# A graph network on one Trainium2 core: the node path's output bias moves from a VectorE add to one-row matmuls in the gather stage

## The reference, cut to what matters

```python
x = h @ W_in.T + b_in
x = jax.nn.silu(x)
x = _linear_diffusion(x, src, dst)
x = x @ W_out.T + b_out
...
x = _layernorm(x + _L3_gnn_ref(...), axis=-1)
```

## Time and profile before

| what | value |
|---|---|
| median of three runs | 3779.49 us |
| the profiled execution | 3806.31 us |
| its span, first to last instruction | 3804.5 us |
| PE busy | 3222.5 us (85% of the span) |
| DVE busy | 2782.3 us (73%) |
| POOL busy | 2084.1 us (55%) |
| ACT busy | 1886.4 us (50%) |
| mean granted TensorE clock | 0.938 |

### The profile page before, as it was taken

One profiled execution on the slowest core, in us unless ns is written; L12 is line 12 of the kernel. 1 busy time (PEld: TensorE's weight loads), 2 busy tenths in 40 slices (PEclk: granted clock), 3 DMA queues, 4 the chain that ended last, 5 costly groups with the idle time before them and its releaser, 6 DMA issues. The chain is left out here.

```text
span 3804.5 us, 56930 instructions
## 1 busy us (share of the span) xinstructions
PE 3222.5 (85%) x15070; PEld 2659.1 (70%) x15070; DVE 2782.3 (73%) x7844; ACT 1886.4 (50%) x5403; POOL 2084.1 (55%) x2118
## 2 busy tenths in 40 slices
PE   5999935588577599856999996999999999999775
PEld 4888824476466366534888885888888787878664
DVE  5666667699688366675677665989989898989742
ACT  3777724466433112134333332666666566666565
POOL 3666600267267566424333333767677676767577
PEclk8999967799799899978999998999999999999997
DMA  4877839644267332247343333878878686868664
GB/s 139 242 242 238 242 106 302 225 128 133 67 197 219 96 89 88 59 145 234 95 125 121 120 119 117 242 210 235 240 212 251 194 252 198 252 200 248 198 218 162
DMA packets 677043, 684.78 MB, mean 180 GB/s; under 512 B 72882, under 2 KB 631015, under 8 KB 676627
## 3 DMA queue, kind: packets, MB, share of 16 engines
q1 hardware_dynamic: 592122, 484.38, 40.8%
q0 software_dynamic: 68160, 181.21, 17.5%
q10 hardware_dynamic: 16444, 15.55, 1.2%
HBM read 401.66 MB, written 283.11 MB: 180 GB/s over the span
## 5 line engine op out<-in xcount | busy, mean ns | idle before, releaser
L2823 PE MATMUL s_i_bank<-s_i_messages,s_i_equal 128*128 128x256 f32 x1200 | 360.5, 383 | 6.9 <-issue 4.4
L622 POOL DMA_INDIRECT s_i_messages<-h,table_row x300 | 305.6, 1019 | 98.0 <-issue 80.8
L932 POOL TENSOR_TENSOR n_powers<-n_powers,neg_half 128x8 f32<-128x8 f32 (+3 forms) x164 | 268.0, 1634 | 165.6 <-issue 59.3
L622 POOL DMA_INDIRECT s_i_messages<-h,table_row_b x300 | 309.2, 1031 | 90.1 <-issue 81.8
L857 ACT ACTIVATE n_z<-gamma_bc,n_powers 128x256 f32<-128x256 f32 x320 | 175.0, 594 | 354.9 <-POOL n_powers L932 354.0
L816 PE MATMUL s_n_bank<-w,n_xt 128*128 128x256 f32 x1280 | 309.1, 385 | 17.8 <-DMA n_xt<-in_x_t 16.8
L834 PE MATMUL s_n_bank<-w_out,n_ht 128*128 128x256 f32 x1280 | 314.0, 390 | 6.5 <-ACT n_ht L844 6.3
L825 PE MATMUL s_n_bank<-n_x3t,w_in 128*128 128x256 f32 x1280 | 303.3, 380 | 0.0
L2852 DVE SCALAR_TENSOR_TENSOR s_i_y<-s_i_bank,s_i_scale,acc 128x256 f32<-128x256 f32 x600 | 285.6, 477 | 5.0 <-remote 5.0
L816 PEld LDWEIGHTS s_n_bank<-w,n_xt 128*128 128x128 f32 x1280 | 246.9, 193 | 53.7 <-DMA n_xt<-in_x_t 17.2
L834 PEld LDWEIGHTS s_n_bank<-w_out,n_ht 128*128 128x128 f32 x1280 | 248.5, 195 | 46.5 <-ACT n_ht L844 11.7
(11 more groups left out here) (452 smaller groups left out, 9268.8 us busy)
## 6 DMA issues: line engine op xcount, KB each, us to landing
h<-s_i_y SPq DMA_DIRECT2D x600, 128.0 KB
n_xt<-in_x_t SPq DMA_DIRECT2D x160, 256.0 KB
out<-n_w SPq DMA_DIRECT2D x160, 256.0 KB
s_i_equal<-eq_tab SPq DMA_DIRECT2D x600, 64.0 KB
x<-s_x_rows SPq DMA_DIRECT2D x100, 256.0 KB
out<-s_a_hs SPq DMA_DIRECT2D x100, 128.0 KB
proj_dst<-s_a_hd SPq DMA_DIRECT2D x100, 128.0 KB
h<-s_h_rows SPq DMA_DIRECT2D x50, 256.0 KB
```

What stands on the lines that cost most here:

```text
L622: return net.nc.gpsimd.indirect_dma_start(out, None, table, bass.IndirectOffsetOnAxis(index, 0))
L932: self.nc.gpsimd.tensor_tensor(v[:, 8 + b0:8 + b1], v[:, b0:b1], self.net.neg_half[:, 0:b1 - b0], ALU.pow).then_inc(self.powered, 1)
L2823: nc.tensor.matmul(banks[r % 4][:, 0:D], EQ[q % NM][:], M[q % NM][:], start=True, stop=True).then_inc(summed, 1)
```

## The change

`Dense` gets a flag `bias_pe`, set in the gather stage alone. With it, `out_project` issues, ahead of the two matmuls of each of its two tiles, one matmul of a single row of ones (1x128) against the single row `b_out` (1x256), which opens the accumulation; the second add of `add_out` is left out, and `square_w` waits for the first add instead. The diffusion stage's 160 units keep the two adds. Other lines move by up to four: in the changed kernel the bias matmul is L834, the output projection L836 and the first add L881.

```diff
-    def __init__(self, net, ctx, tag, first, units):
+    def __init__(self, net, ctx, tag, first, units, bias_pe=False):
...
-        self.first = first
+        self.first, self.bias_pe = first, bias_pe
...
         for g in range(self.G):
+            if self.bias_pe:
+                self.nc.tensor.matmul(self.op[:, g * self.D:(g + 1) * self.D], self.net.ones[0:1, :], self.net.bc["b_out"][0:1, :], start=True, stop=False)
             for m in range(self.C):
                 mm = self.nc.tensor.matmul(self.op[:, g * self.D:(g + 1) * self.D], self.HT[:, m, g * P:(g + 1) * P], self.net.w_out[:, m, :],
-                                           start=m == 0, stop=m == self.C - 1)
+                                           start=m == 0 and not self.bias_pe, stop=m == self.C - 1)
...
-        act.wait_ge(self.w_ready, j * 2 + (u + 1))
+        act.wait_ge(self.w_made if self.bias_pe else self.w_ready, j * 2 + (u + 1))
...
         V.tensor_tensor(self.W[u][:], self.op[:, :].rearrange("p (g d) -> p g d", g=self.G), self.X3[u][:], ALU.add).then_inc(self.w_made, 1)
+        if self.bias_pe:
+            return
         dve.wait_ge(self.w_made, j * 2 + (u + 1))
         V.tensor_tensor(self.W[u][:], self.W[u][:], self.net.bc["b_out"][:].unsqueeze(1).broadcast_to([P, self.G, self.D]), ALU.add).then_inc(self.w_ready, 1)
...
-        dn = Dense(net, st.ctx, "m", 0, net.early)
+        dn = Dense(net, st.ctx, "m", 0, net.early, bias_pe=True)
```

## The result

| what | before | after |
|---|---|---|
| median of six runs each | 3780.81 us (3779.07 to 3786.25) | 3797.91 us (3794.62 to 3805.61) |
| ratio of the runs | | 1.0042, 95% interval 1.0031 to 1.0054 |
| the profiled execution, its span | 3806.31, 3804.5 us | 3805.61, 3803.8 us |
| gather stage | 304.4 us | 323.4 us |
| head / 27 turns of the middle / tail | 35.9 / 189.5 / 79.0 us | 38.9 / 196.2 / 88.3 us |

The change makes the kernel 0.42% slower: 0.0042 x 3780.8 = 15.9 us. It goes from the first matmul of `project` to the first matmul of the diffusion stage; the head ends at the first power that is eight values wide, the middle is the 27 intervals between the 28 powers from there, the tail is the rest.

A forecast was written before the change was run, and what follows sets the result against it. The prediction took a loop through POOL, ACT and DVE, without the bias add, to bound the middle. Middle +0.6, head +1.7 and tail +3.7 made +6.0 on 3779.5, so 3785.5 us; the range was 3778 to 3802.

The forecast's parts named there:

- first rival: PE's stream breaks at each change of height, 1.65 us a turn, PE becomes the bound; +19, 3798.5 us, chance 0.34.
- forecast: Whole kernel: one-row matmuls at 1.17 us a turn nearly fit PE's idle time; +6.0, 3785.5 us, chance 0.50.
- What bounds the middle: Middle of the gather stage: a loop through POOL, ACT and DVE without the bias add; removing adds gives 0.
- second rival: DVE is the bound after all: 28 turns give back 0.69 each, 19.3 less; -13.9, 3765.6 us, chance 0.07.
- The records: Added matmuls on PE: four records a turn at 0.216 us each, 0.87 us; fewer rows are no cheaper.
- The breaks: PE's flow at changes between one row and 128 rows: three a turn at 0.10 us, 0.30 in all.
- my upper bound: Dearest price on PE: three breaks of 0.26 us, 0.79 a turn, making 1.65 in all.
- PE's room: Middle: time PE can fill before it bounds the turn, 1.15 to 1.29 us; 1.25 in the first rival.
- the point of decision: Middle: the first rival decides from a price of about 1.25 us a turn on.
- Tail: End of the stage: four turns, each price plus 0.3 for breaks minus 0.69, together +3.7 us.
- Head: Start of the stage: first output projection delays the PE work behind it, 1.4 plus 0.3 for breaks, +1.7 us.
- Third rival: Tail: longer pieces keep PE's clock up, slow groups come down to 1.89 us; -0.6, 3778.9 us, chance 0.09.

The follow-up runs named there:

- e2: The changed kernel with the bias matmuls left out too, so the gather stage adds no output bias; 3778.10 us, 0.9981 of the kernel before.
- e7: The changed kernel with 65 rows of ones against 65 rows of `b_out` instead of one; 3786.78 us, 1.0002 of the kernel before.
- e1: The changed kernel with full-height bias matmuls, 128x128 identity against `b_out` in all 128 rows, same place; 3781.65 us, 0.9996 of the kernel before.
- e6: The changed kernel with 64 rows of ones against 64 rows of `b_out` instead of one; 3804.03 us, 1.0051 of the kernel before.
- e5: The changed kernel with one one-row bias matmul of 512 columns for both tiles instead of two of 256; 3789.09 us, 1.0015 of the kernel before.
- e3: The changed kernel with the second add kept as well, so the bias counts twice; 3802.21 us, 1.0047 of the kernel before.

## Why the prediction was right or wrong

The range held the time, and the case that came is the **first rival**, to which I gave 0.34: 3798.5 us predicted, 3797.9 measured. The forecast, 3785.5, was the wrong case. Point by point:

- **What bounds the middle: right.** "I take 0 for them there": without the adds the middle loses 0.8 us of 189.5 (e2). The second rival, 19.3 us back, is refuted although DVE was 91% busy.
- **The records: right.** 0.43 us for two in flow, at 65 or 128 rows alike (e7, e1); two of one row never stand in flow.
- **The breaks: the step that failed.** "I take the one kind of break that the trace shows by itself, 0.10, three times." Measured in the turn of after against the flow of e1: 0.10 on the way in, 0.20 behind the first bias, 0.20 ahead of the second, 0.19 behind it, 0.10 in the last four records; 0.79 in all. The price is 0.53 + 0.63 + 1.06 + 0.62 + 0.97 less the flow of transposes and projection (0.43 + 1.73), 1.65 us a turn, not 1.17. The weight loads show where the time lies (timeline of PEld in after, a turn in which the bias doesn't wait, its matmuls as far apart as in the middle):

```profile
1024.45 0.29 PEld L834 LDWEIGHTS s_m_bank<-b_out_bc,ones 1*128 1x128 f32 x2 [0.33 <-issue]
1025.08 0.73 PEld L836 LDWEIGHTS s_m_bank<-w_out,m_ht 128*128 128x128 f32 x4 [0.33 <-issue]
1025.83 1.70 PEld L825 LDWEIGHTS s_m_bank<-m_x3t,w_in 128*128 128x128 f32 x8
```

`hidden` (L825) loads its weights from 1025.83 on, 0.21 ahead of its first matmul at 1026.04. The bias and the projection begin to load only when their own first matmul starts, at 1024.45 and 1025.08. So a break costs about 0.10 ahead of the meeting (the way in) and 0.10 behind it, where the load is no longer hidden: 0.20, of which I had taken half. And there are four of them, two a visit, not three, as no bias of the middle stands behind a wait any more. That my upper bound's three of 0.26 make the same 0.79 is chance. What misled me was the earlier trace rows: a 65-row matmul seemed the nearest row to a one-row one and flowed. It was near in shape and far in kind, as e6 and e7 show.
- **PE's room: a size off.** I had 1.25 us. A turn of PE without idle is 3 x 1.73 + 0.43 = 5.62, so the room is 7.04 - 5.62 = 1.42. The idle time in a row counts from the modelled end of the transposes, 0.62 behind their start, though the next piece can start 0.43 behind it; these 0.19 were missing. So the rival's 0.40 a turn is 1.65 - 1.42 = 0.23, the 7.26 of the trace, and its 11.2 us of the middle are 6.6. e5 brackets the point of decision: 1.26 keeps 7.04, 1.65 does not.
- **Tail: sign right, size off.** +3.7 predicted, +9.4 measured, and much the same with 64 rows (+8.2) or the add kept (+10.1). The first three turns, counted with the middle at next to nothing, grew by 0.42, 0.79 and 0.74. The four that I costed came to 6.6 together; 0.8 of the 9.4 is in neither. The largest, at 993.42, is costed at +0.85 and came to +2.4: the bias and the projection take 6.17 us in after (999.50 to 1005.67) where the projection alone took 3.06 before, and one add of 0.69 is saved.

Timeline of PE after, that turn:

```profile
998.51 1.06 PE L680 MATMUL s_m_bank<-ident,m_x 128*128 128x128 f32 x4
999.50 1.22 PE L834 MATMUL s_m_bank<-b_out_bc,ones 1*128 1x256 f32 x2
1000.65 2.08 PE L836 MATMUL s_m_bank<-w_out,m_ht 128*128 128x256 f32 x4
1002.65 1.22 PE L834 MATMUL s_m_bank<-b_out_bc,ones 1*128 1x256 f32 x2
1003.80 2.08 PE L836 MATMUL s_m_bank<-w_out,m_ht 128*128 128x256 f32 x4
1005.67 2.60 PE L825 MATMUL s_m_bank<-m_x3t,w_in 128*128 128x256 f32 x8
```

The starts of a bias and its projection are 1.15 and 2.00 us apart, where the middle has 0.63 and 1.06. The granted clock of this turn (busy time by stretch, columns as above; the clock is the third number from the end), in the kernel before:

```profile
991.79:996.48 4.69, 4.69 (x16) 4.10 (x17) 2.67 (x8) 1.39 (x5) 0.55 (x1) 0.54 0.02 5
996.48:999.40 2.92, 2.49 (x13) 1.75 (x11) 2.65 (x8) 1.80 (x4) 1.09 (x1) 1.00 0.00 0
```

and in the kernel after:

```profile
997.73:1005.67 7.94, 7.94 (x20) 5.12 (x21) 2.67 (x8) 3.49 (x10) 1.64 (x1) 0.50 0.00 0
1005.67:1008.70 3.03, 3.03 (x13) 2.35 (x11) 2.60 (x9) 1.07 (x1) 0.00 (x0) 0.76 0.27 92
```

The first stretch of each begins where PE starts again after idle time (6.28 us before, 5.39 after). Before, the clock is at full speed by the end of the projection; now the whole piece and part of `hidden` run at half (1.2 GHz). I had let it rise within the group. The breaks go with that, and not the longer piece (e7, then e6, the same matmuls from the same place on, with 65 and with 64 rows of bias):

```profile
980.86:987.20 6.34, 6.34 (x20) 5.39 (x21) 2.67 (x8) 1.91 (x7) 1.64 (x1) 0.53 0.00 0
994.55:1002.49 7.94, 7.94 (x21) 5.12 (x21) 2.67 (x8) 3.50 (x10) 1.64 (x1) 0.50 0.00 0
```

With 65 rows the clock is up before the piece ends, with 64 it is not.
- **Head: not settled.** +1.7 predicted; after has +3.0, e6 -0.2, e3 -2.0 with the same price, and the kernels without breaks lie between 33.1 and 35.9. One profile of each can't tell it.
- **Third rival: refuted.** The tail's groups got longer, not shorter.

The first rival's sum was near partly by chance: its middle was 11.2 (6.6 came), its ends 7.9 (12.4 came).

## What to carry to other kernels

A small matmul put between large ones is not priced by its records alone: at 1 and at 64 rows it cost 0.40 us a visit here, at 65 or 128 rows nothing beyond its columns. So a bias is added by an identity of full height against the bias in all rows, in one visit, and issued where PE would idle. And before work moves from the busiest engine to another, see whether the adds it frees stood in anyone's way: 24.9 us of DVE were worth 4.9 us of the stage.

## What the runs showed of the hardware that was not expected

- The break has a threshold between 64 and 65 rows and is the same at the two heights below it that were run: 0.62 to 0.63 us to the next start at 1 and at 64 rows, 0.43 to 0.44 at 65 and 128.
- At half clock a pair of visits costs more: between the transposes at 998.51 and `hidden` at 1005.67 the starts are 0.99, 1.15, 2.00, 1.15 and 1.87 us apart; at twice the 0.43, 0.43, 0.86, 0.43 and 0.87 of full clock they would be 0.86, 0.86, 1.72, 0.86 and 1.74, so 1.12 us instead of 0.79.
- In the same turn the four kernels with breaks had the clock at half for 7.94 us (after, e3, e6) or 7.35 (e5, one visit) and on into `hidden`; in the six without it had risen before `hidden`, at the latest in e7, within 6.34, with as many records and columns as e6. PE had been idle about as long ahead of it in both groups (5.39 us in after, 5.38 in e1 and e6, 5.92 in e7). It is one execution of each kernel.
